# Eight-maxima gates, an earlier second half of f2, and expert 0's weights spread from token-major weights

## The chip, the cores and the metric

The kernel runs on one core of a Trainium2 chip. Such a core has TensorE (PE) for matrix products into PSUM banks, VectorE (DVE), ScalarE (ACT), GpSimd (POOL) and SyncE (SP), the last of which here only starts transfers. Each engine runs its own instructions in order and waits for others by semaphores. The metric is the time on the device in microseconds (us), the median of several runs; lower is better.

## The reference, cut to what matters

The program adds four blocks to a stream `x` of 8 batches of 100 tokens of width 256. Each block works on the layer norm of the stream and is weighted by the tanh of a gate: a cross attention, a top-1 mixture of experts, a text block with ternary weights (`bitnet_linear`: inputs rounded to 8 bits, one scale for the whole tensor), and a mixture-of-experts attention with 16 experts. The change lies at the end of the third block and in the start of the fourth:

```python
h = jax.nn.relu(bitnet_linear(concatenated, W_f1, b_f1))
return bitnet_linear(h, W_f2, b_f2)          # end of block 3; x = x + tanh(g) * this
# block 4, on x = layernorm(x), n = 800 tokens, E = 16 experts, MIN_E = 2
xn = x / jnp.maximum(jnp.linalg.norm(x, axis=-1, keepdims=True), 1e-12)
logits = xn @ sn - jax.nn.sigmoid(gates)
gated = jax.nn.relu(logits)
hard = (gated > 0).astype(gated.dtype)
inactive = jnp.sum(hard, axis=1) == 0        
_, fb_idx = jax.lax.top_k(logits, MIN_E)     # then the two best are put in
...
w = jax.nn.softmax(masked, axis=-1)          # over the active experts
y = jnp.einsum('nc,ech->neh', x, p)          # for p in q_proj, k_proj, v_proj
... = jnp.einsum('ne,neh->nh', w, y)
# then attention within a batch, and the 16 output projections, again weighted by w
```

## The kernel before

Block 4 is done in two halves of 4 batches (400 tokens, `HT`). The order on every engine is that of the code; there is no scheduler. Names ending in `_mm`, `_out`, `_in`, `_done` are semaphores.

**The layer f2.** The 8-bit form of h is made by `round_hidden` on VectorE and by a loop on ScalarE, one instruction for each of 8 row tiles and each half; `OWN` says how many tiles of each half VectorE takes (5 and 3), and ScalarE takes the others. `second_product(b)` multiplies batch b: one matmul for an offset, and eight over the tiles, which for b = 0 and b = 4 wait tile by tile. Its result goes to the bank and column of `RESULT[b]`. `third_residual(h)` adds the results to x on VectorE and takes statistics.

**The fourth norm and its turn.** `last_variance`, `last_normalise` and `token_norm` (VectorE) and `last_layernorm` (ScalarE) normalise; each engine does two batches of a half. `turn_half` transposes the normalised tokens on PE into two banks, and ScalarE copies these to `xT`.

**Gates.** `gate_scores` (PE) forms the logits, 100 tokens by 4x16. VectorE's `gate_logits`, `gate_second` and `gate_weights` make the weights w: the largest logit, the softmax's numerator, the second largest by masking the first out (ties go to the lower index, by a descending constant `rev16`), and the division. `link` makes an instruction's successors wait until it is through.

**Weights to the projections.** `turn_weights` transposes w to expert-major, ScalarE copies it to `wT`, and POOL stores it to DRAM and reads it back broadcast over 128 partitions (`w_bc`) in the groups of experts of `GROUPS`. Experts 0 and 1 of the first half do not wait for that: `spread_weights(e)` multiplies a broadcast unit column with `wT`, and VectorE copies the result to `w_bc` and multiplies the tokens with it straight from PSUM (`weigh_tokens`). `project(h, e)` adds expert e's three projections: 6 matmuls of 400 columns, which show as 12 rows in a trace, since a product in f32 is two instructions (a transpose is one). There are three buffers of weighted tokens (`NW`) and four of expert matrices (`NP`).

`keep_busy(bank, n)` is filler: n matmuls with constants whose result nobody reads. 

## Time and profile before

| | us |
|---|---|
| median of 3 runs | 611.05 |
| lowest, highest | 610.5, 611.07 |
| span of the profiled execution | 608.3 |

The profiled execution's own time is not given beside its span; the median is 2.75 us longer than the span.

| engine | busy us | share |
|---|---|---|
| PE, matmuls | 591.7 | 97% |
| DVE | 326.1 | 54% |
| ACT | 218.1 | 36% |
| POOL | 76.4 | 13% |

A row of a timeline gives the start, the time covered, the engine, the line of the code, the operation with its operands and shapes, and the count; in brackets the idle time ahead of it and what ended it. Filler counts as busy. The clock granted to PE is a share of full speed; the page's mean over the span is 0.992.

### The profile page before, as it was taken

The page shows a single profiled execution, that of the slowest core. Times are in us where ns is not written, and L with a number is a line of the kernel's source. Part 1 is how long each engine was busy: PE and PEld are TensorE (multiplying, and loading weights), DVE is VectorE, ACT ScalarE, POOL GpSimd, SP SyncE. Part 2 cuts the span into 40 slices and gives each one's busy share as a digit, 9 for nine tenths or more (in the row PEclk, how much of TensorE's full clock was granted, in tenths as well). Part 3 has the DMA queues.
Part 4 walks back from the last instruction along what each step waited for, and adds up shares of the span by engine and source line. Part 5 has one row for each costly group of instructions (what it writes and reads, how often), then busy time and mean ns, then how long its engine had stood idle before and what let it go on. Part 6 is the DMA issues. An engine that isn't in the chain of part 4 may idle for free.

```text
span 608.3 us, 9635 instructions
## 1 busy us (share of the span) xinstructions
PE 591.7 (97%) x3765; PEld 404.7 (67%) x3765; DVE 326.1 (54%) x787; ACT 218.1 (36%) x511; POOL 76.4 (13%) x75
## 2 busy tenths in 40 slices
PE   9999999999999989999999899999999999999997
PEld 7755344554556758999999568677655555555587
DVE  2896767697876664222222879976362223131454
ACT  3554665666664373111112575761200010001100
POOL 0052100022006102222231000001001000000000
PEclk9999999999999999999999799998999999999999
DMA  8910000102001645989994001501733833320000
GB/s 192 325 75 5 15 1 1 37 2 57 1 1 40 237 158 182 332 345 339 344 350 168 1 1 50 194 1 27 246 101 89 310 104 91 91 78 1 0 28 27
DMA packets 25580, 70.63 MB, mean 116 GB/s; under 512 B 5255, under 2 KB 13031, under 8 KB 21703
## 3 DMA queue, kind: packets, MB, share of 16 engines
q1 hardware_dynamic: 21910, 58.16, 29.0%
q0 software_dynamic: 3632, 11.97, 6.0%
q8 instruction: 25, 0.41, 0.3%
q14 instruction: 13, 0.10, 0.0%
HBM read 64.62 MB, written 5.49 MB: 115 GB/s over the span
## 4 chain that ended last, share of the span: by engine, by line
PE 84%; DVE 7%; ACT 5%; DMA 2%; issue 1%; POOL 1%; SPq 1%; DVEq 0%
PE bank L2115 21%; PE bank L1608 10%; PE bank L1935 8%; PE bank L1948 8%; PE bank L1761 7%; PE bank L2151 7%; PE bank L1735 5%; PE bank L1779 3%; DMA region<-in_ctxT 2%; PE bank L1704 2%; ACT region L1500 2%; PE bank L1767 2%; PE bank L2069 2%; PE bank L1589 1%; DVE nmax L1033 1%
## 5 line engine op out<-in xcount | busy, mean ns | idle before, releaser
L2115 PE MATMUL bank<-region,kvT 128*128 128x400 f32 x384 | 130.4, 500 | 0.0
L2115 PEld LDWEIGHTS bank<-region,kvT 128*128 128x128 f32 x384 | 72.4, 190 | 54.2 <-issue 0.3
L731 DVE TENSOR_REDUCE nmax<-bank 100x2 f32<-100x722 f32 x64 | 55.2, 905 | 24.9 <-PE bank L1735 24.6
L1174 DVE TENSOR_TENSOR region<-xT,stage 128x800 f32<-128x800 f32 x30 | 29.7, 991 | 70.0 <-PE bank L2115 69.9
L1935 PEld LDWEIGHTS bank<-stage,region 128*128 128x128 f32 x448 | 52.1, 192 | 1.4 <-issue 0.8
L1935 PE MATMUL bank<-stage,region 128*128 128x128 f32 x448 | 52.4, 275 | 0.5 <-ACT stage L1435 0.5
L1948 PE MATMUL bank<-region,stage 128*128 128x256 f32 x224 | 50.7, 379 | 0.0
L1948 PEld LDWEIGHTS bank<-region,stage 128*128 128x128 f32 x224 | 41.5, 190 | 5.1
L2151 PE MATMUL bank<-region,kvt 128*128 128x200 f32 (+1 forms) x192 | 44.5, 389 | 0.3 <-DVE region L1200 0.3
L1458 ACT ACTIVATE stage<-bank,stage 128x128 f32<-128x128 f32 x56 | 16.0, 368 | 66.5 <-PE bank L1935 61.1
L2151 PEld LDWEIGHTS bank<-region,kvt 128*128 128x128 f32 x192 | 33.5, 190 | 9.3 <-DVE region L1200 0.6
L947 DVE TENSOR_SCALAR stage<-bank,stage 128x128 f32<-128x128 f32 x56 | 15.8, 344 | 43.1 <-PE bank L1935 43.1
L1761 PE MATMUL bank<-xT,kvt 64*121 64x400 f32 (+1 forms) x144 | 37.9, 545 | 0.7 <-ACT region L1414 0.3
L1200 DVE TENSOR_TENSOR region<-region,stage 128x200 f32<-128x200 f32 (+1 forms) x48 | 20.5, 435 | 31.3 <-PE bank L2151 31.3
L1414 ACT ACTIVATE region<-bank 121x400 f32<-121x400 f32 (+1 forms) x48 | 21.8, 501 | 19.8 <-PE bank L1767 19.8
L1414 ACT ACTIVATE kvT<-bank 121x400 f32<-121x400 f32 (+1 forms) x48 | 21.8, 501 | 19.2 <-PE bank L1767 19.2
L953 DVE TENSOR_TENSOR stage<-bank,stage 128x256 f32<-128x256 f32 x14 | 5.9, 425 | 35.6 <-PE bank L1948 35.6
L1735 PE MATMUL bank<-kvt,xT 32*100 32x361 f32 x192 | 23.2, 502 | 1.2 <-POOL xT L473 0.7
L1761 PEld LDWEIGHTS bank<-xT,kvt 64*121 64x121 f32 (+1 forms) x144 | 13.3, 178 | 13.8 <-ACT region L1414 3.6
L1536 ACT ACTIVATE region<-bank 128x400 f32<-128x400 f32 x6 | 2.6, 504 | 55.5 <-PE bank L2115 55.5
L1608 PE MATMUL bank<-w_a,region 96*121 96x256 f32 (+1 forms) x96 | 22.1, 380 | 0.0
L1608 PE MATMUL bank<-region,w_a 96*128 96x361 f32 x64 | 21.2, 475 | 0.9 <-ACT xn L1327 0.7
(352 smaller groups left out, 932.2 us busy)
## 6 DMA issues: line engine op xcount, KB each, us to landing
region<-in_e_w SPq DMA_DIRECT2D x28, 1024.0 KB, 5.9
kvT<-in_p_qkv SPq DMA_DIRECT2D x32, 384.0 KB, 3.1
stage<-w_dram POOLq DMA_DIRECT2D x2, 1600.0 KB, 12.7
stage<-in_t_f SPq DMA_DIRECT2D x1, 2048.0 KB, 14.7
kvt<-in_p_o SPq DMA_DIRECT2D x1, 2048.0 KB, 9.6
stage<-in_e_b SPq DMA_DIRECT2D x14, 128.0 KB, 7.2
region<-in_ctxT SPq DMA_DIRECT2D x3, 541.5 KB, 14.3
stage<-w_dram POOLq DMA_DIRECT2D x1, 1200.0 KB, 8.8
```

What stands on the lines that cost most here:

```text
L731: dve.tensor_reduce(nmax[:, b % 2, at_h:at_h + 9:8], banks[0:N, bank:bank + 2, 0:M], AX.X, ALU.max, negate=True)\
L1174: dve.tensor_tensor(x_w[n % NW], xT[:, :, at_h], w_bc[h][:, None, e, :].to_broadcast([P, 2, HT]), ALU.mult).then_inc(S["xw_done"], 1)
L1200: dve.tensor_tensor(z_w[n % NW][:, at_p], oT[h][:, at_p], w_bc[h][:, e, at_p], ALU.mult)\
L1414: act.activation(probsT[n % 2][0:rows_c, c, g].rearrange("p j n -> p (j n)"), psum[4 + y % 3][0:rows_c, 0:4 * N], ACT.Exp).then_inc(S["y_o ...
L1608: ins = pe.matmul(bank, w(k), src(k), start=start and k == 0, stop=stop and k == kk - 1)
L1735: ins = pe.matmul(psum[i + (4 if b == 0 else 0)][0:N, 0:M], qm[b % 3][at_i, t, 2 * (i % 2) + par, :], kT[at_i, t, b, :], start=True, stop= ...
L1761: pe.matmul(bank[g], kT[at_g, t, b, c0:c0 + rows_c], qm[b % 3][at_g, t].rearrange("p j n -> p (j n)"), start=True, stop=False)
L1779: ins = pe.matmul(psum[7][32 * i:32 * i + VW, w * N:(w + 1) * N], v_b[b][0:rows_c, c, 8 * t + 2 * i + par, :], probsT[b % 2][0:rows_c, c, ...
L1935: ins = pe.matmul(psum[2 * u + m // 4][:, (m % 4) * P:(m % 4 + 1) * P], e_w1[u][:, k, m * P:(m + 1) * P], xsT[u][:, k, :], start=k == 0, s ...
L1948: ins = pe.matmul(psum[4 + u][:, 0:D], hsT[u][:, m, :], e_w2[u][:, m, :], start=m == 0, stop=m == KF - 1)
L2115: ins = pe.matmul(psum[3 * h + j][:, 0:HT], p_w[n % NP][:, k, j * HE:(j + 1) * HE], x_w[n % NW][:, k, :], start=e == 0 and k == 0, stop=e ...
L2151: ins = pe.matmul(psum[LAST_BANK[part] + m][:, at_p], o_all[:, e, m * P:(m + 1) * P], z_w[n % NW][:, at_p], start=e == 0, stop=e == E1 - 1)
```

## The change

- **Rounding.** `OWN` becomes (5, 0): ScalarE rounds all of the second half. f2's output scale is worked out on VectorE after its rounding, no longer ahead of it.
- **Products.** Seven of the eight f2 products stand ahead of the turn of the normalised tokens, with the banks of batches 4 to 7 exchanged; one stands behind the gate scores. The filler between the fourth product and the turn is gone.
- **Copy.** The second of the two turned banks of the first half is copied by VectorE.
- **Gates.** The largest eight logits of a token and their positions come from `max` and `max_index`, four of each per half (one per batch). The second gate is put in by comparing positions with a counting constant, to which 128 is added where the largest logit is above zero, so that then nothing matches.
- **Spreading.** `spread_weights` multiplies the token-major weights, one column broadcast to 128, with the identity: 4 matmuls of 100 columns in place of one of 400, and no need of `wT`. Expert 0's tokens are weighted in two parts, and `project_first` starts on the first, with expert 1's spreading between its halves. The rows of `w_bc` for experts 0 and 1 now come by a fourth broadcast on POOL's queue, which `weigh_heads` waits for.
- **A semaphore.** `w_2`'s load counts on the semaphore of `w_1`.

The first place is PE's queue around f2. Before, L2062 and L2069 are a product's offset and its eight tiles, L1589 filler, L2082 the turn, L1608 the gate scores:

```order
L2062 MATMUL bank<-stage 100x256
L2069 MATMUL bank<-tern,region 100x256 x8
L1589 MATMUL bank<-consts 128x256 x7
L2082 MATMUL bank<-consts,xn 128x100 x8
L1589 MATMUL bank<-consts 128x256
L1608 MATMUL bank<-sim,xT 100x16 x8
L2062 MATMUL bank<-stage 100x256
L2069 MATMUL bank<-tern,region 100x256 x8
L2062 MATMUL bank<-stage 100x256
```

After the change, from the fifth product on, the same things are on L2047 and L2054, L1575, L2067 and L1594:

```order
L2047 MATMUL bank<-stage 100x256
L2054 MATMUL bank<-tern,region 100x256 x8
L2047 MATMUL bank<-stage 100x256
L2054 MATMUL bank<-tern,region 100x256 x8
L2047 MATMUL bank<-stage 100x256
L2054 MATMUL bank<-tern,region 100x256 x8
L2067 MATMUL bank<-consts,xn 128x100 x8
L1575 MATMUL bank<-consts 128x256
L1594 MATMUL bank<-sim,xT 100x16 x8
L2047 MATMUL bank<-stage 100x256
L2054 MATMUL bank<-tern,region 100x256 x8
```

Three products have moved from behind the gate scores to ahead of the turn, in the place of seven filler calls.

The second place is PE's queue around the weights. Before, L2099 turns them, L2105 spreads, L2115 projects (18 calls are three experts):

```order
L2069 MATMUL bank<-tern,region 100x256 x8
L1589 MATMUL bank<-consts 128x256 x5
L2099 MATMUL bank<-consts,small 16x100 x4
L1589 MATMUL bank<-consts 128x256
L2105 MATMUL bank<-w_a,consts 128x400 x2
L1589 MATMUL bank<-consts 128x256 x2
L2115 MATMUL bank<-region,kvT 128x400 x18
```

After the change, the turn is on L2084, the spreading on L2091, expert 0's projection on L2101, the others' on L2114:

```order
L2054 MATMUL bank<-tern,region 100x256 x8
L1575 MATMUL bank<-consts 128x256 x4
L2084 MATMUL bank<-consts,small 16x100 x4
L2091 MATMUL bank<-consts,small 128x100 x4
L2101 MATMUL bank<-region,kvT 128x400 x3
L2091 MATMUL bank<-consts,small 128x100 x4
L2101 MATMUL bank<-region,kvT 128x400 x3
L2114 MATMUL bank<-region,kvT 128x400 x12
```

The fillers around the spreading are gone, and the second spreading has moved into the first projection.

The third place is VectorE's queue in the gates. Before, from the first comparison with zero; `r_a` to `r_d` are per-token numbers, `small` holds the logits and masks:

```order
L1113 TENSOR_SCALAR small<-small 100x64
L1114 TENSOR_REDUCE r_b<-small 100x4
L1115 TENSOR_SCALAR small<-small 100x64
L1116 TENSOR_TENSOR small<-small,r_b 100x64
L1117 TENSOR_SCALAR r_d<-r_b 100x4
L1118 TENSOR_TENSOR small<-small,r_d 100x64
L1120 TENSOR_REDUCE r_a<-small 100x4
L1121 TENSOR_SCALAR r_a<-r_a 100x4
L1132 TENSOR_TENSOR small<-small,consts 100x64
L1133 TENSOR_REDUCE r_b<-small 100x4
L1134 TENSOR_TENSOR small<-small,r_b 100x64
L1135 SCALAR_TENSOR_TENSOR small<-small 100x64
```

and 12 more follow until the weights are done. After, from the eight maxima on:

```order
L1113 MAX top<-small 100x8 x4
L1115 TENSOR_SCALAR small<-small 100x64
L1116 TENSOR_SCALAR r_d<-top 100x4
L1117 TENSOR_SCALAR far<-top 100x4
L1118 TENSOR_TENSOR small<-small,r_d 100x64
L1120 TENSOR_TENSOR small<-consts,far 100x64
L1122 TENSOR_SCALAR small<-small 100x64
L1124 MAX_INDEX top_at<-top,small 100x8 x4
L1131 TENSOR_TENSOR small<-small,top_at 100x64 x2
L1134 TENSOR_REDUCE small<-small 100x64
```

and 4 follow. The chain of linked small reductions has gone; MAX and MAX_INDEX stand four times each.

The diff, without the removed constant, the new tiles, the lists of semaphores and most of the removed `gate_second`:

```diff
--- before.py
+++ after.py
@@ -36,7 +36,7 @@
-OWN = (5, 3)
+OWN = (5, 0)
...
@@ -46,8 +46,8 @@
-RESULT = ((0, 0), (1, 0), (2, 0), (3, 0), (3, 0), (3, D), (6, 0), (6, D))
-GROUPS = (((2, 4), (4, 8), (8, 16)), ((0, 2), (2, 8), (8, 16)))
+RESULT = ((0, 0), (1, 0), (2, 0), (3, 0), (6, 0), (6, D), (3, 0), (3, D))
+GROUPS = (((2, 4), (4, 8), (8, 16), (0, 2)), ((0, 2), (2, 8), (8, 16)))
...
@@ -380,7 +382,7 @@
             sp.wait_ge(S["pv_mm"], 3)
-            sp.dma_start(w_2, d["w_2"]).then_inc(S["w1_small_in"], 16)
+            sp.dma_start(w_2, d["w_2"]).then_inc(S["ffn_in"], 16)
...
@@ -539,7 +541,7 @@
                 pool.wait_ge(S["wT_stored"], 16 * (h + 1))
                 for g, (e0, e1) in enumerate(GROUPS[h]):
                     pool.dma_start(w_bc[h][:, e0:e1], d["w_dram"][None, e0:e1, at_h].to_broadcast([P, e1 - e0, HT]))\
-                        .then_inc(S[f"wb_in{h}{g}"], 16)
+                        .then_inc(S[f"wb_in{h}{g}" if g < 3 else "wb_first"], 16)
...
@@ -1080,9 +1082,6 @@
             dve.tensor_reduce(scol[:, 20:21], umax[:, :], AX.X, ALU.max).then_inc(S["max_part"], 1)
             input_scale(6, 20)
             dve.sem_inc(S["in_scale"], 1)
-            output_scale(20, ("f2",))
-            link(dve.tensor_scalar(scol[:, 28:29], scol[:, 46:47], tg[:, 1:2], None, ALU.mult))
-
             def round_hidden(h, m):
 
...
@@ -1105,56 +1104,41 @@
             def gate_logits(h):
 
                 bs = slice(4 * h, 4 * h + 4)
-                lg_h, a_h, c_h = lg[:, bs, :], l_a[:, bs, :], l_b[:, bs, :]
+                lg_h = lg[:, bs, :]
                 dve.wait_ge(S["lg_mm"], h + 1)
                 link(dve.tensor_tensor(lg_h, psum[7 if h == 0 else 3][0:N, 0:4 * E1].rearrange("p (b e) -> p b e", b=4),
                                        nsq[:, bs, None].to_broadcast([N, 4, E1]), ALU.mult))
                 link(dve.tensor_tensor(lg_h, lg_h, sig[:, None, :].to_broadcast([N, 4, E1]), ALU.subtract))
-                dve.tensor_scalar(a_h, lg_h, 0.0, None, ALU.is_gt)
-                link(dve.tensor_reduce(r_b[:, bs], lg_h, AX.X, ALU.max))
+                for b in range(4 * h, 4 * h + 4):
+                    ins = dve.max(top8[:, b, :], lg[:, b, :])
+                link(ins)
                 dve.tensor_scalar(soft[:, bs, :], lg_h, 0.0, None, ALU.max)
-                dve.tensor_tensor(c_h, lg_h, r_b[:, bs, None].to_broadcast([N, 4, E1]), ALU.is_equal)
-                link(dve.tensor_scalar(r_d[:, bs], r_b[:, bs], 0.0, None, ALU.max))
+                dve.tensor_scalar(r_d[:, bs], top8[:, bs, 0], 0.0, None, ALU.max)
+                link(dve.tensor_scalar(far[:, bs], top8[:, bs, 0], 0.0, float(P), ALU.is_gt, ALU.mult))
                 dve.tensor_tensor(soft[:, bs, :], soft[:, bs, :], r_d[:, bs, None].to_broadcast([N, 4, E1]), ALU.subtract)\
                     .then_inc(S["lg_vec"], 1)
-                link(dve.tensor_reduce(r_a[:, bs], a_h, AX.X, ALU.add))
-                dve.tensor_scalar(r_a[:, bs], r_a[:, bs], 0.0, None, ALU.is_equal)
-
-            def gate_second(h):
+                dve.tensor_tensor(l_d[:, bs, :], const("slot", N)[:, None, 0:E1].to_broadcast([N, 4, E1]),
+                                  far[:, bs, None].to_broadcast([N, 4, E1]), ALU.add)
+                dve.tensor_scalar(l_a[:, bs, :], lg_h, 0.0, None, ALU.is_gt)
+                for b in range(4 * h, 4 * h + 4):
+                    ins = dve.max_index(top_at[:, b, :], top8[:, b, :], lg[:, b, :])
+                link(ins)
+
+            def gate_weights(h):
 
                 bs = slice(4 * h, 4 * h + 4)
-
-                def over(r):
-                    return r[:, bs, None].to_broadcast([N, 4, E1])
-
-                rev = const("rev16", N)[:, None, :].to_broadcast([N, 4, E1])
-                lg_h, first, second, rest = lg[:, bs, :], l_b[:, bs, :], l_c[:, bs, :], l_d[:, bs, :]
...
-            def gate_weights(h):
-
-                bs = slice(4 * h, 4 * h + 4)
-
-                def over(r):
-                    return r[:, bs, None].to_broadcast([N, 4, E1])
-
-                soft_h, a_h, put = soft[:, bs, :], l_a[:, bs, :], l_b[:, bs, :]
-                link(dve.tensor_tensor(put, put, over(r_a), ALU.mult))
-                link(dve.tensor_tensor(a_h, a_h, put, ALU.max))
+                for z in range(2):
+                    ins = dve.tensor_tensor(small[:, 2 + z, bs, :], l_d[:, bs, :],
+                                            top_at[:, bs, z:z + 1].to_broadcast([N, 4, E1]), ALU.is_equal)
+                link(ins)
+                link(dve.tensor_reduce(l_d[:, bs, :], small[:, 1:4, bs, :].rearrange("n z b e -> n b e z"), AX.X, ALU.max))
                 dve.wait_ge(S["lg_exp"], h + 1)
-                link(dve.tensor_tensor(soft_h, soft_h, a_h, ALU.mult))
+                soft_h = soft[:, bs, :]
+                link(dve.tensor_tensor(soft_h, soft_h, l_d[:, bs, :], ALU.mult))
                 link(dve.tensor_reduce(r_b[:, bs], soft_h, AX.X, ALU.add))
                 link(dve.reciprocal(r_b[:, bs], r_b[:, bs]))
-                dve.tensor_tensor(lg[:, bs, :], soft_h, over(r_b), ALU.mult).then_inc(S["w_done"], 1)
+                dve.tensor_tensor(lg[:, bs, :], soft_h, r_b[:, bs, None].to_broadcast([N, 4, E1]), ALU.mult)\
+                    .then_inc(S["w_done"], 1)
 
             def weigh_tokens(h, e):
 
@@ -1164,9 +1148,10 @@
                     dve.wait_ge(S["qkv_mm"], n - NW + 1)
                 if h == 0 and e < 2:
                     dve.wait_ge(S["w0_mm"], e + 1)
-                    dve.tensor_copy(w_bc[0][:, e, :], psum[4 + e][:, 0:HT])
-                    dve.tensor_tensor(x_w[n % NW], xT[:, :, at_h], psum[4 + e][:, None, 0:HT].to_broadcast([P, 2, HT]),
-                                      ALU.mult).then_inc(S["xw_done"], 1)
+                    for ks in (slice(0, 1), slice(1, 2)) if e == 0 else (slice(0, 2),):
+                        dve.tensor_tensor(x_w[n % NW][:, ks, :], xT[:, ks, at_h],
+                                          psum[4 + e][:, None, 0:HT].to_broadcast([P, ks.stop - ks.start, HT]), ALU.mult)\
+                            .then_inc(S["xw_done"], 1)
                     return
                 for g, (e0, _) in enumerate(GROUPS[h]):
                     if e == e0:
@@ -1195,6 +1180,8 @@
                 n, (h, at_p) = E1 * part + e, LAST_PART[part]
                 if e == 0 and part < 2:
                     dve.wait_ge(S["o_ready"], h + 1)
+                if n == 0:
+                    dve.wait_ge(S["wb_first"], 16)
                 if n >= NW:
                     dve.wait_ge(S["out_mm"], n - NW + 1)
                 dve.tensor_tensor(z_w[n % NW][:, at_p], oT[h][:, at_p], w_bc[h][:, e, at_p], ALU.mult)\
@@ -1209,14 +1196,15 @@
 
             for m in range(OWN[0]):
                 round_hidden(0, m)
-            for m in range(OWN[1]):
-                round_hidden(1, m)
+            output_scale(20, ("f2",))
+            link(dve.tensor_scalar(scol[:, 28:29], scol[:, 46:47], tg[:, 1:2], None, ALU.mult))
             third_residual(0)
             last_variance(0)
             last_normalise(0)
             token_norm(0)
+            dve.wait_ge(S["ln_turned"], 14)
+            dve.tensor_copy(xT[:, 1, 0:HT], psum[5][:, 0:HT]).then_inc(S["xT_ready"], 1)
             gate_logits(0)
-            gate_second(0)
             gate_weights(0)
             weigh_tokens(0, 0)
             weigh_tokens(0, 1)
@@ -1229,8 +1217,6 @@
                 weigh_tokens(0, e)
                 if e == 4:
                     gate_logits(1)
-                if e == 5:
-                    gate_second(1)
                 if e == 6:
                     gate_weights(1)
             for e in range(E1):
@@ -1516,7 +1502,7 @@
                 for b in range(4 * h + 2, 4 * h + 4):
                     act.activation(xn[:, b, :], x[:, b, :], ACT.Identity, bias=var[:, b:b + 1],
                                    scale=rstd[:, b:b + 1]).then_inc(S["ln_act"], 1)
-                for kk in range(2):
+                for kk in range(h + 1):
                     act.wait_ge(S["ln_turned"], 12 + 2 * h + kk + 1)
                     act.copy(xT[:, kk, h * HT:(h + 1) * HT], psum[(4 if h == 0 else 6) + kk][:, 0:HT])\
                         .then_inc(S["xT_ready"], 1)
@@ -1833,7 +1819,7 @@
                 if n == B:
-                    pe.wait_ge(S["ffn_in"], 32)
+                    pe.wait_ge(S["ffn_in"], 48)
                     pe.wait_ge(S["x_max"], 8 * B)
                     first_product(0, 0)
...
@@ -2057,7 +2042,7 @@
             def second_product(b):
 
                 bank, at = RESULT[b]
-                if b == 4:
+                if b == 6:
                     pe.wait_ge(S["x3_done"], 4)
...
@@ -2102,14 +2087,28 @@
 
             def spread_weights(e):
 
-                pe.matmul(psum[4 + e][:, 0:HT], ident[0:E1, e:e + 1].to_broadcast([E1, P]), wT[:, 0:HT],
-                          start=True, stop=True).then_inc(S["w0_mm"], 1)
+                for b in range(4):
+                    ins = pe.matmul(psum[4 + e][:, b * N:(b + 1) * N], lg[:, b, e:e + 1].to_broadcast([N, P]),
+                                    ident[0:N, 0:N], start=True, stop=True)
+                ins.then_inc(S["w0_mm"], 1)
+
+            def project_first():
+
+                pe.wait_ge(S["p_in0"], 16)
+                for k in range(2):
+                    pe.wait_ge(S["xw_done"], k + 1)
+                    for j in range(3):
+                        ins = pe.matmul(psum[j][:, 0:HT], p_w[0][:, k, j * HE:(j + 1) * HE], x_w[0][:, k, :],
+                                        start=k == 0, stop=False)
+                    if k == 0:
+                        spread_weights(1)
+                ins.then_inc(S["qkv_mm"], 1)
 
             def project(h, e):
 
                 n = E1 * h + e
                 pe.wait_ge(S[f"p_in{n % NP}"], 16 * (n // NP + 1))
-                pe.wait_ge(S["xw_done"], n + 1)
+                pe.wait_ge(S["xw_done"], n + 2)
                 for j in range(3):
                     for k in range(2):
                         ins = pe.matmul(psum[3 * h + j][:, 0:HT], p_w[n % NP][:, k, j * HE:(j + 1) * HE],
@@ -2166,23 +2165,20 @@
 
             pe.wait_ge(S["f2_sums"], 1)
             keep_busy(0, 7)
-            for b in range(4):
+            for b in range(7):
                 second_product(b)
-            keep_busy(6, 7)
             turn_half(0)
-            keep_busy(6, 1)
+            keep_busy(0, 1)
             gate_scores(0)
-            for b in range(4, B):
-                second_product(b)
-            keep_busy(0, 5)
+            second_product(7)
+            keep_busy(0, 4)
             turn_weights(0)
-            keep_busy(0, 1)
-            pe.wait_ge(S["wT_out"], 1)
             spread_weights(0)
-            spread_weights(1)
-            keep_busy(0, 2)
             for e in range(E1):
-                project(0, e)
+                if e == 0:
+                    project_first()
+                else:
+                    project(0, e)
                 if e == 2:
                     turn_half(1)
                 if e == 3:
```

## Rows read from the trace of the kernel before

**Rows 1.** The page: its head, and the engines' shares of the chain that ended last.
```profile
span 608.3 us, 9635 instructions
...
PE 84%; DVE 7%; ACT 5%; DMA 2%; issue 1%; POOL 1%; SPq 1%; DVEq 0%
```
**Rows 2.** Timeline of PE, 396 to 423 us.
```profile
396.45 3.19 PE L1589 MATMUL bank<-consts 128*128 128x256 f32 x14
...
407.69 1.42 PE L2082 MATMUL bank<-consts,xn 100*128 100x100 f32 x8
...
409.74 1.58 PE L1608 MATMUL bank<-sim,xT 128*100 128x16 f32 x16 [0.18 <-ACT xT L1521]
411.17 0.29 PE L2062 MATMUL bank<-stage 128*100 128x256 bf16 x1
...
412.89 0.42 PE L2062 MATMUL bank<-stage 128*100 128x256 bf16 x1
...
414.81 0.28 PE L2062 MATMUL bank<-stage 128*100 128x256 bf16 x1
...
416.79 2.32 PE L1589 MATMUL bank<-consts 128*128 128x256 f32 x10
418.95 0.51 PE L2099 MATMUL bank<-consts,small 100*16 100x100 f32 x4
...
420.03 1.60 PE L2105 MATMUL bank<-w_a,consts 16*128 16x400 f32 x4
...
422.61 12.33 PE L2115 MATMUL bank<-region,kvT 128*128 128x400 f32 x36
```
**Rows 3.** One microsecond within the products behind the scores, with the granted clock (PEclk).
```profile
core 0: us, PE busy (x) PEld busy (x) DVE busy (x) ACT busy (x) POOL busy (x), PEclk, DMA share, GB/s
412.00:413.00 1.00, 1.00 (x7) 0.97 (x6) 0.93 (x7) 0.00 (x0) 0.00 (x0) 0.50 0.00 0
```
**Rows 4.** Timeline of DVE, 399 to 428 us.
```profile
399.12 0.21 DVE L632 TENSOR_SCALAR scol<-ws,scol 128x1 f32<-128x1 f32 x1 [0.16 <-DVE scol L627]
...
399.62 2.79 DVE L1089 TENSOR_SCALAR region<-region,scol 128x400 bf16<-128x400 f32 x8
...
406.04 0.38 DVE L598 BATCH_NORM_AGGREGATE mv<-stats 100x2 f32<-100x6 f32 x4
...
411.44 0.23 DVE L1110 TENSOR_TENSOR small<-bank,nsq 100x64 f32<-100x64 f32 x1 [3.03 <-PE bank L1608]
...
411.95 0.20 DVE L1113 TENSOR_SCALAR small<-small 100x64 f32<-100x64 f32 x1
412.06 0.21 DVE L1114 TENSOR_REDUCE r_b<-small 100x4 f32<-100x64 f32 x1
412.31 0.20 DVE L1115 TENSOR_SCALAR small<-small 100x64 f32<-100x64 f32 x1
...
417.04 0.22 DVE L1157 TENSOR_TENSOR small<-small,r_b 100x64 f32<-100x64 f32 x1
421.00 0.57 DVE L1167 COPY stage<-bank 128x400 f32<-128x400 f32 x1 [3.73 <-PE bank L2105]
421.49 0.98 DVE L1168 TENSOR_TENSOR region<-xT,bank 128x800 f32<-128x800 f32 x1
...
423.76 0.87 DVE L1098 SCALAR_TENSOR_TENSOR x<-bank,scol,x 100x256 f32<-100x256 f32 x2
...
427.35 0.99 DVE L1174 TENSOR_TENSOR region<-xT,stage 128x800 f32<-128x800 f32 x1
```
**Rows 5.** Timeline of ACT: the rounding, and the copies of the turned tokens.
```profile
399.06 5.00 ACT L1506 ACTIVATE region<-region,scol 128x400 bf16<-128x400 f32 x8 [1.73 <-DVEq L1082]
...
408.80 0.89 ACT L1521 COPY xT<-bank 128x400 f32<-128x400 f32 x2 [0.40 <-PE bank L2082]
```
**Rows 6.** Chain that ended last: start, us, what; f32 matmuls of 128x128 elsewhere.
```profile
238.02 3.57 PE bank L1935 x32
```
**Rows 7.** Timeline of POOL: the broadcasts of the first half.
```profile
422.37 2.44 POOL L541 DMA_DIRECT2D stage<-w_dram  x3 [1.53 <-DMA w_dram<-w_a]
```

19 lines of the change are left out of this document (5 added, 14 removed).

## The prediction

> **What bounds the kernel now.** I read the page first: a span of 608.3 us, and a chain that ended last which is 84% TensorE [rows 1]. So time can come only from where TensorE waits or works on filler. The timeline of PE around the change shows both between the last text layer and the expert projections [rows 2]. Read it downwards: filler (L1589) until 399.47, the products of layer f2 (L2062, L2069), a second batch of filler, the turn of the normalised tokens at 407.69, the gate scores at 409.74, four more f2 products from 411.17, filler from 416.79, the turn of the gate weights at 418.95, the spreading at 420.03, and the first projection at 422.61. From there PE does not wait again until 556: the rows L2115 stand back to back, 36 instructions in 12.33 us or 0.34 us each. Whatever brings the start of expert 1's projection forward therefore comes off the end; what happens on VectorE or ScalarE counts only ahead of that point. The second half of the work (the second turn, scores and gates) lies under projections.
>
> One more thing is in [rows 2]: the four f2 products after the gate scores are not equal. The first takes 411.17 to 412.89 and the second 1.92 us, while the third and fourth take 0.99 us each (414.81 to 416.79). The row of that stretch says why [rows 3]: the granted clock is 0.50, so PE is at 1.2 GHz; it had just done the turn and the scores, many instructions with 100 or 16 columns and gaps. This costs before some 1.8 us on the path, and it is why the weights, finished on VectorE at 417.26 [rows 4], were picked up only at 418.95.
>
> **Part 1, rounding.** VectorE now rounds 5 tiles and computes f2's output scale behind them. The scale is known to both engines at about 399.06 (ACT starts then, [rows 5]), VectorE begins at 399.62 [rows 4]; the two small linked instructions between go behind, so rounding starts 0.5 us earlier. The first f2 product waits for the fifth tile, and the three behind it follow at 0.98 us each: all shift by 0.5, and the fourth product ends at 404.2, where a second batch of filler, now gone, stood behind it.
>
> **Part 2, three more products before the turn.** ScalarE now rounds 11 tiles instead of 8 at 5.00/8 = 0.625 us [rows 5]: the last is ready at 399.06 + 6.88 = 405.94. The fifth product wants it last, so PE waits some 0.8 us in it and goes on at 406.1. Two more products (0.99 each) end at 408.05. The normalised tokens would be ready for a turn at about 407.2 (407.69 less 0.5), the last of them at 407.9; so the turn starts 0.35 later than before but runs without its waits: 8 transposes took 1.42 us with waits, I take 0.86 without. That gives 408.9, plus 0.15 until the last result is out. ScalarE is free at 405.94, and wants to be by 406.1 for the standard deviations: covered by little.
>
> **Part 3, the copy of the turned tokens.** It took two ScalarE copies in sequence, 0.89 us from 408.80 [rows 5]. Now VectorE, idle there, does the second; 128x400 out of PSUM is 0.57 us [rows 4]. 409.05 + 0.57 + 0.05 gives gate scores at 409.70, before 409.74. Parts 1 to 3 together thus move the scores by nothing worth naming: the half microsecond and the parallel copy pay for three products moved ahead of them. VectorE's gates start at 411.40.
>
> **Part 4, what is left for PE behind the scores.** One product and 8 filler instructions (4 calls) instead of four products and 10. If the clock drops as before, the product ends at 412.85; filler takes 3.02/14 = 0.216 at full clock and twice that at half, so 4.5 of the 8 fit until 414.8 and the rest ends at 415.56. Without the drop it is 414.0.
>
> **Part 5, the gates on VectorE.** Before: 27 instructions in 5.82 us (411.44 to 417.26, [rows 4]), one linked to the next costing 0.25 us from start to start (412.06 to the next), one unlinked 0.11 (411.95 to 412.06), a small one in a row 0.07 (4 BN_AGGREGATE in 0.38). Now: two linked 0.51; four MAX over 16 values 3x0.08 + 0.25 = 0.49; three small 0.38; three 64-wide unlinked 0.39; four MAX_INDEX; two compares 0.39; a maximum over 3x64 values 0.39 (estimated from 0.21 at 64 elements and about 1 ns per further one, as 0.57 at 400 says); and the unchanged end, 0.95. MAX and MAX_INDEX have no row in this trace. The least is a small instruction's 0.07 to 0.08, the most the 0.57 us of the 128x400 copy [rows 4], far off in size. I take the near end, 0.08, and to be careful count an index operation double, since it has eight values to compare with besides the 16 it reads: 8x0.08 + 0.17 = 0.81. Sum 4.31 us, weights done at 415.71. With everything at 0.07 it is 0.1 less; at 0.25 for each of the 12 it would be 2.0 us more.
>
> A row cannot tell how many instructions an index operation is. The Trainium skill, "Vector Engine (DVE) Microarchitecture Reference", section 3.9, says that positions are found by a separate pair, one instruction that loads the eight values and one that searches: this speaks against the change by four instructions per half, some 0.3 us at the small row's pitch. By one instruction each, the weights would be done at 415.4.
>
> **Part 6, spreading without ScalarE.** Before, from the turn of weights to the first projection: turn 418.95, copy on ScalarE, spread at 420.03, VectorE at 421.00 copies (0.57) and multiplies (0.98), projection at 422.61: 3.66 us. Now the turn starts at 415.78 (weights at 415.71; PE has been free since 415.56) and takes 0.34. The spread of expert 0 follows at once: 4 calls, 8 f32 instructions; 32 such of 128x128 take 3.57 us [rows 6], 0.112 each, 0.89 together, out at 417.2. VectorE multiplies only half of the tokens' rows, 0.57, so PE starts at 417.94. The first projection then has the spread of expert 1 inside: 6x0.34 + 0.89 + 6x0.34 = 4.97, and expert 1's begins at 422.91. Before, it began at 422.61 + 12x0.34 = 426.69. **Gain: 3.78 us.** It comes from PE's queue (3.2 us earlier at the turn) and the shorter way (0.5 net of the spread in the projection).
>
> **What is late next.** Expert 1's tokens: its spread ends at 421.0, VectorE's 0.98 makes it 422.1, 0.8 in time. Then VectorE does the third residual's second half and statistics, 423.76 to 427.35 before [rows 4], now 422.05 to 425.65, and expert 2's product until 426.64; PE wants it at 422.91 + 4.08 = 426.99. In time by 0.3. Expert 2's weights come by POOL's DMA: issued 422.37 [rows 7] and read at 427.35 [rows 4], so at most 4.98 under way; now 3.2 us earlier, landed by 424.2. The extra load for experts 0 and 1 (400 KB) is last in POOL's queue for this half and wanted only after all 32 projections, 130 us later. Half 1's gates get shorter under cover: nothing. The load of w_2, now behind the same semaphore as w_1, is far ahead of its use: nothing. The 16 constant columns: nothing.
>
> **Sum.** The profiled span is 608.3 us; less 3.8 it is 604.5. The median of the runs is 611.05, 2.75 above the span, and I carry that: 611.05 - 3.8 = **607.2 us**.
>
> **Rivals.** (a) *The clock falls a second time.* Before, PE's stretch 415 to 422 was full of filler; now it is transposes, narrow spreads and 0.8 us of waiting before the projection. If the clock goes to half for as long as after the scores (411.2 to 414.8, 3.6 us), of which 3.5 fall on projections, these lose 1.75: gain 2.0, 609.0 us. For it: the drop seen came right after such work. Against: there is 1 us of filler at the start and a full projection from 417.94 on. The Trainium skill ("TensorE: Matmul & The Clock Gate", part 4) says that transposes don't count as PE being busy, which would make the four turns here idle time too and this rival more likely; nothing in the rows separates them from the 16-column scores. 13%. The same drop in the fifth product's wait (0.8 us) would halve two products and the turn: 609.6 us, 4%.
> (b) *MAX and MAX_INDEX are middling dear*, 0.2 us each: 1.3 us more, 608.5 us. For it: no row. 9%.
> (c) *Slower than before*: VectorE's gate chain becomes the bound by these twelve instructions. PE waits for it from the start, so each 0.1 us of price costs 1.2; the gain of 3.78 is eaten at 0.08 + 3.78/12 = 0.40 us each. At the far end, 0.57, it is 5.9 - 3.8 = 2.1 us slower, and PE's idle wait would bring the half clock as well, up to 1.75: 613 to 615. Against: they read 16 values, and a reduction over 64 values, linked, costs 0.25 [rows 4]. 4%.
> (d) *The gain is hidden*: expert 2's product or weights come late (0.3 us and 1.4 us in hand), PE stalls at 427 and gives back up to 3: about 610.2. 4%.
>
> **How the numbers follow.** The forecast has 66%, its own range 606.4 to 608.2: less time if the clock does not drop and VectorE is quick, more by small waits. The range 606.2 to 609.4 takes in (b) and most of (a). Within 0.2%, the least this kernel's measurement can tell, is 609.8 to 612.3: (d), a part of (a) and (c), 0.08; slower 0.04; faster 0.88.
>
> **What would show it.** In the profile after: rounding on VectorE from 399.1; a wait of about 0.8 us in the fifth product; scores at 409.7; MAX at 0.07 to 0.1 from start to start and the chain of gates about 4.3 us; filler ending just before the turn of weights at 415.8; spread at 0.11 per instruction; first projection at about 417.9 and then no wait of PE until the end. The forecast is wrong if the gate chain takes over 5 us, if the clock column shows a half behind 416, or if PE waits for VectorE at expert 2.

## The result

| | runs | median, us | lowest, highest |
|---|---|---|---|
| before | 14 | 611.06 | 609.3, 614.67 |
| changed | 14 | 609.14 | 607.66, 610.73 |

The ratio is 0.997, with a 95% interval of 0.9956 to 0.9983: faster by 1.9 us at the medians, 1.0 to 2.7 by the interval. The forecast was 607.2 with a gain of 3.8. The sign held, and 609.14 lies within the whole range of 606.2 to 609.4, but outside the 606.4 to 608.2 to which I had given 66%: the gain was half of what I worked out.

A puzzle stands at the start: the changed kernel's profiled execution, 610.73 us itself and the slowest of its 14, has a longer span than that of before.

```profile
span 608.9 us, 9618 instructions
...
PEclk9899999999999998999999899999999999999999
...
PE 84%; DVE 7%; ACT 5%; DMA 2%; issue 1%; SPq 1%; DVEq 0%; POOL 0%
```

The page's head, clock line and chain shares answer to [rows 1]. The timeline of PE in the same profile, from the filler behind f1 on, answers to [rows 2]:

```profile
401.16 3.19 PE L1575 MATMUL bank<-consts 128*128 128x256 f32 x14
...
410.66 0.31 PE L2054 MATMUL bank<-tern,region 128*100 128x256 bf16 x1 [0.19 <-ACT region L1492]
...
412.77 0.85 PE L2067 MATMUL bank<-consts,xn 100*128 100x100 f32 x8
...
414.36 1.58 PE L1594 MATMUL bank<-sim,xT 128*100 128x16 f32 x16 [0.28 <-DVE xT L1206]
415.79 0.29 PE L2047 MATMUL bank<-stage 128*100 128x256 bf16 x1
...
416.79 1.89 PE L1575 MATMUL bank<-consts 128*128 128x256 f32 x8
420.20 0.51 PE L2084 MATMUL bank<-consts,small 100*16 100x100 f32 x4 [1.52 <-DVE small L1140]
420.55 1.06 PE L2091 MATMUL bank<-consts,small 100*128 100x100 f32 x8
422.36 2.25 PE L2101 MATMUL bank<-region,kvT 128*128 128x400 f32 x6 [0.76 <-DVE region L1152]
...
427.36 8.22 PE L2114 MATMUL bank<-region,kvT 128*128 128x400 f32 x24
```

Two things are to be read here. The filler behind f1 starts at 401.16 where it started at 396.45 before: this execution had lost 4.7 us ahead of the stretch that the change is about. (Ahead of it the diff touches only the constants' table, theory C below, the semaphore of one load and the tiles reserved.) And from there to expert 1's projection it takes 26.20 us, where before it took 30.24 (396.45 to 426.69, by the working of part 6): the change did save 4.0 us in this stretch. Below, "the stretch" is measured from the start of f1's last matmul, 0.17 ahead of that filler, to the start of expert 1's first: 30.4 us in before's profile, 26.4 here. Behind it, every one of the 14 profiles that I have of all kernels here takes 181.5 us to its end, within 0.05. So the last part holds no loss and no gain.

The clock tells the rest. Before had its half clock behind the gate scores ([rows 3]); here it stays full there, so the one product takes 1.0 us and PE comes to the weights 1.52 us early. The view by windows shows it; its columns are the window, its length, then busy time and count of PE, PEld, DVE, ACT and POOL, the mean granted clock (1.00 is 2.4 GHz, 0.50 is 1.2 GHz), the DMA share and GB/s:

```profile
411.00:423.00 12.00, 9.45 (x75) 8.17 (x74) 6.86 (x37) 5.05 (x9) 0.57 (x1) 1.00 0.01 4
```

VectorE's gates, from the timeline of DVE in the changed kernel:

```profile
415.98 0.22 DVE L1109 TENSOR_TENSOR small<-bank,nsq 100x64 f32<-100x64 f32 x1 [1.68 <-PE bank L1594]
...
416.50 0.41 DVE L1113 MAX8 top<-small 100x8 f32<-100x16 f32 x4
416.94 0.20 DVE L1115 TENSOR_SCALAR small<-small 100x64 f32<-100x64 f32 x1
...
417.69 0.08 DVE L1124 MATCH_VALUE_LOAD top_at<-top,small 100x8 f32 x1
417.76 0.17 DVE L1124 FIND_INDEX8 top_at<-top,small 100x8 uint32<-100x16 f32 x1
417.85 0.07 DVE L1124 MATCH_VALUE_LOAD top_at<-top,small 100x8 f32 x1
...
418.40 0.36 DVE L1131 TENSOR_TENSOR small<-small,top_at 100x64 f32<-100x64 f32 x2
418.79 0.37 DVE L1134 TENSOR_REDUCE small<-small 100x64 f32<-100x192 f32 x1
...
419.92 0.22 DVE L1140 TENSOR_TENSOR small<-small,r_b 100x64 f32<-100x64 f32 x1
```

These rows answer to [rows 4]. The gates take 415.98 to 420.14, 4.16 us; four MAX take 0.44 from start to the next instruction, and each index operation is two instructions, 0.16 from one pair to the next (417.69, 417.85). The two that had no row, MAX and MAX_INDEX, were priced right.

So the question is not whether the 4.0 us are there, but where 2 of them go in the other executions.

### The profile page after: what moved, and what is told of

The parts are those of the page before. It is cut to its first block, busy times and chain, and to the rows that moved or that the text cites. A ratio compares the mean times of both kernels' runs of the same rounds, so it can differ in the third digit from the quotient of the medians.

```text
span 608.9 us, 9618 instructions
## 1 busy us (share of the span) xinstructions
PE 589.6 (97%) x3755; PEld 403.6 (66%) x3755; DVE 322.1 (53%) x786; ACT 220.1 (36%) x513; POOL 77.2 (13%) x76
## 3 DMA queue, kind: packets, MB, share of 16 engines
q1 hardware_dynamic: 21910, 58.15, 29.3%
## 4 chain that ended last, share of the span: by engine, by line
PE 84%; DVE 7%; ACT 5%; DMA 2%; issue 1%; SPq 1%; DVEq 0%; POOL 0%
PE bank L2114 21%; PE bank L1594 11%; PE bank L1920 8%; PE bank L1933 8%; PE bank L1747 7%; PE bank L2150 7%; PE bank L1721 5%; PE bank L1765 3%; DMA region<-in_ctxT 2%; PE bank L1690 2%; ACT region L1486 2%; PE bank L1753 2%; ACT region L1492 1%; DVE nmax L1035 1%; PE bank L1575 1%; DVE stage L1046 1%
## 5 line engine op out<-in xcount | busy, mean ns | idle before, releaser
L2114 PE MATMUL bank<-region,kvT 128*128 128x400 f32 x372 | 126.3, 500 | 0.0
L2114 PEld LDWEIGHTS bank<-region,kvT 128*128 128x128 f32 x372 | 70.2, 190 | 52.5
L1594 PE MATMUL bank<-region,w_a 96*128 96x361 f32 x64 | 22.9, 505 | 2.6 <-DMA region<-in_ctxT 1.9
L1594 PE MATMUL bank<-w_a,region 96*121 96x256 f32 (+1 forms) x96 | 22.1, 380 | 0.0
```

The lines of the kernel that those rows point to most:

```text
L1594: ins = pe.matmul(bank, w(k), src(k), start=start and k == 0, stop=stop and k == kk - 1)
L2114: ins = pe.matmul(psum[3 * h + j][:, 0:HT], p_w[n % NP][:, k, j * HE:(j + 1) * HE], x_w[n % NW][:, k, :], start=e == 0 and k == 0, stop=e ...
```

## The experiments

Three theories. **S**: the stretch saves 4.0 every time, and the scatter of what lies ahead of it hides this. **W**, named F in the first expectation: the saving itself differs between executions. It took its full form only after the first three runs: the stretch has more than one price in each kernel, by where the clock falls. Before is at 28.8, plus 1.6 when it falls behind the gate scores, as in its first profile; the changed kernel is at 26.4, plus up to 3 when it falls over the first projections, since PE waits twice just ahead of them. **C**: the constants' table, 16 columns shorter, makes the start slower. Each kernel ran 10 to 12 times, and one of these runs was profiled.

### Before, again

> The kernel before, unchanged: a second profile of it. Theory S (the change saves 4.0 us between the end of layer f1 and the projection of expert 1 in every execution, and the rest of what the times show comes from ahead of it): the stretch from the first filler behind f1 to the first row of expert 1's projection is 30.2 us again when the clock falls to half behind the gate scores, and about 28.7 when it does not, since PE then reaches the weights at 417.4 instead of 418.95. The span varies by what the start (transfers of the context, first 40 us) and the stretch 210 to 235 us cost. Rival F (the saving itself differs between executions): the stretch is 28.7 or less in this profile, so that the change is worth 2.5 or less in many executions.

611.36 us at the median of 10 (ratio to before 1.0012, 0.9986 to 1.0037). Its timeline of PE behind the scores:

```profile
418.56 2.32 PE L1589 MATMUL bank<-consts 128*128 128x256 f32 x10
420.75 0.51 PE L2099 MATMUL bank<-consts,small 100*16 100x100 f32 x4
...
424.42 5.95 PE L2115 MATMUL bank<-region,kvT 128*128 128x400 f32 x17
```

The scores began at 413.18, so the four products were through in 5.38 us with them; before's first profile took 7.05 (409.74 to 416.79, [rows 2]). The clock was full: the stretch is 28.8. So the half clock behind the scores is a matter of the execution, and with it 1.6 us of my gain: against this execution the change saves 2.4, not 4.0.

### Changed, again

> The changed kernel, unchanged: a second profile of it. Theory S: the same stretch takes 26.2 us again, whatever the clock does behind the scores. If the execution starts as that of before did (first transpose of the tokens at 23.6 and not 26.8 us) and has no half clock near 230, its span is about 604.5. Rival C (the shorter constants make the start slower): the first transpose is late again, near 26 to 27 us.

610.14 us at the median of 10 (0.9984, 0.9957 to 1.001). The stretch is 26.4. The first transpose of the tokens stands at 24.7; in the changed kernel's first profile it was at 26.8, in before's two at 23.7 and 24.1. So that slow start is not a fixed cost of the change (C). This profile alone cannot tell W from S.

### Changed, with the constants kept

```diff
-                  ("bounds", OVER), ("base", E0), ("rev8", E0), ("over", OVER),
+                  ("bounds", OVER), ("base", E0), ("rev8", E0), ("rev16", E1), ("over", OVER),
```

> The changed kernel with the 16 constant columns kept, so that the constants' transfer (128 x 620 numbers) and all addresses behind it are those of before. Rival C: the start is that of before (first transpose near 23.6) and the time is 2 us lower than the changed kernel's, about 607.2. Theory S: no difference, under 0.7 us either way.

608.7 us (0.9966, 0.9944 to 0.9989), which looked like C. But its profile shows what I had given 13%, here the timeline of PE:

```profile
416.32 0.51 PE L2085 MATMUL bank<-consts,small 100*16 100x100 f32 x4 [1.52 <-DVE small L1141]
416.67 1.06 PE L2092 MATMUL bank<-consts,small 100*128 100x100 f32 x8
418.48 4.34 PE L2102 MATMUL bank<-region,kvT 128*128 128x400 f32 x6 [0.75 <-DVE region L1153]
422.61 1.87 PE L2092 MATMUL bank<-consts,small 100*128 100x100 f32 x8
```

and the granted clock over it, in the view by windows for 417.8 to 424.6:

```profile
417.80:424.60 6.80, 6.12 (x15) 4.17 (x16) 1.10 (x3) 0.85 (x1) 3.56 (x5) 0.50 0.46 113
```

The six half products take 4.34 us in place of 2.25, and the spreading 1.87 in place of 1.03. PE is at 1.2 GHz for 6.8 us; before that it had waited 1.52 us and done narrow transposes and spreads, and the second wait, 0.75 us, had just begun (417.73). The stretch is 29.4: 3.0 more than without, more than the 1.75 of rival (a), since the fall lasted twice as long as the one I took it from.

### Only the new gates

```diff
-            gate_second(0)
...
-                if e == 5:
-                    gate_second(1)
```

with `gate_logits` and `gate_weights` of the changed kernel, all else of before.

> The kernel before with only the new gates (MAX and MAX_INDEX). The weights are done 1.5 us earlier on VectorE (4.2 instead of 5.8 us of chain), but PE's products and filler end at 418.95 relative to the same start, so the span stays: no difference within 0.3 us, unless the clock does not fall, where before is bound by filler too (417.4) and it is again 0.

611.07 us (1.0022, 0.9997 to 1.0047): no gain, as expected. The gates end 1.65 us sooner (4.17 against 5.82), and PE picks the weights up when its filler ends.

```profile
417.13 2.32 PE L1574 MATMUL bank<-consts 128*128 128x256 f32 x10
419.29 0.51 PE L2084 MATMUL bank<-consts,small 100*16 100x100 f32 x4
```

Its stretch is 30.4, with the half clock behind the scores again.

### More filler

```diff
-            keep_busy(0, 4)
+            keep_busy(0, 7)
             turn_weights(0)
             spread_weights(0)
+            keep_busy(0, 1)
```

> The changed kernel with three more filler calls ahead of the turn of the weights (7 instead of 4, in the 1.5 us in which PE waited for the weights when the clock was full) and one call behind expert 0's spreading (0.43 us, in the 0.76 us wait). Stretch = last row of f1's products to the first of expert 1's projection; it was 30.4 and 28.8 us in two profiles of before, 26.4, 26.4 and, in one with a half clock from 417.8 to 424.6, 29.4 in three of the change. Theory W (the changed order leaves PE so idle between 414 and 422 that in some executions the clock falls over the first projections, 3 us each time): no half clock there, the stretch is 26.4 to 26.6 or, where the clock falls behind the scores, up to 27.7; median time 0.5 to 1.5 us below the changed kernel's, ratio to before about 0.995. Rival S (the stretch always saves 4.0 and the rest is the start's scatter): no difference from the changed kernel, or slower by the filler.

608.53 us (0.997, 0.995 to 0.999), stretch 26.4, no half clock there. Its median is 0.6 and 1.6 below those of the changed kernel in its two earlier sets; none ran beside it: W's direction, but within the scatter.

### No filler

```diff
-            keep_busy(0, 4)
             turn_weights(0)
```

> The changed kernel without the 4 filler calls ahead of the turn of the weights: PE then waits 3.2 us there. Theory W: the clock falls over the projections in most executions; stretch about 29.4, median 2 us above the changed kernel's, near before's time. Rival S: the weights are the bound, the filler is only cover: stretch 26.4 and the same time.

612.18 us (1.0025, 1.0001 to 1.0049), some 3 us above the changed kernel's first median (from another set), though the kernel does less. The weights come as before; the wait for them is 3.25 us, and the clock falls ahead of the turn:

```profile
417.61 0.83 PE L2084 MATMUL bank<-consts,small 100*16 100x100 f32 x4 [3.25 <-DVE small L1140]
418.24 1.91 PE L2091 MATMUL bank<-consts,small 100*128 100x100 f32 x8
420.90 4.34 PE L2101 MATMUL bank<-region,kvT 128*128 128x400 f32 x6 [0.75 <-DVE region L1152]
```

```profile
415.70:425.90 10.20, 7.54 (x23) 5.25 (x24) 2.70 (x10) 1.76 (x2) 3.72 (x5) 0.50 0.25 55
```

Above is the timeline of PE, below it the same view by windows over the half clock, 10.2 us long. The stretch is 30.0. S is out, as it was with e3's 29.4: filler is not only cover here; without it the clock fell. The runs without a profile say the same: their mean clock over the span is 0.977 to 0.988 in all 12, where 28 of the 58 runs of the changed kernel (constants kept or not) have 0.989 or more.

### Only the f2 order

```diff
-            for b in range(4):
+            for b in range(7):
                 second_product(b)
-            keep_busy(6, 7)
             turn_half(0)
```

with the rounding, the copy and, up to the turn of the weights, the filler of the changed kernel; gates and spreading of before, with its fillers around the spreading.

> The kernel before with only the f2 order, the rounding, the copy and the fewer fillers; old gates and old spreading. By my terms: weights done at 5.8 us of chain (relative 417.2), turn there instead of 418.95, then the old 3.66 us to the projection with its fillers: stretch 28.8, 1.6 less than before where the clock falls behind the scores, 0 to 0.2 less where it does not.

614.47 us (1.0052, 1.0026 to 1.0079): slower than before by 3.4 at the medians (before has 611.03 in this set). The long gates now leave PE waiting 3.17 us, and the clock is at half from 421.9 to 428.7:

```profile
416.22 1.89 PE L1588 MATMUL bank<-consts 128*128 128x256 f32 x8
421.29 0.51 PE L2098 MATMUL bank<-consts,small 100*16 100x100 f32 x4 [3.17 <-DVE small L1154]
421.64 0.83 PE L1588 MATMUL bank<-consts 128*128 128x256 f32 x2
422.39 3.03 PE L2104 MATMUL bank<-w_a,consts 16*128 16x400 f32 x4
```

I expected a stretch of 28.8; it is 31.6. The turn comes 20.9 after f1's last matmul, and the 7.8 of the old way behind it (418.95 to 426.7 in before) would give 28.7: my terms hold, and 2.9 is the clock. It was a miss of the same kind as the prediction's.

### Gates and spreading, old f2 order

> The changed kernel with the old f2 order, rounding, copy and filler. PE's products and filler end when they did, so the turn is at the old place and the shorter gates give nothing; the new spreading saves 0.6: stretch 29.8 with a half clock behind the scores, 28.2 without. With e7: neither part alone gives the 4.0, the new gates pay only behind the new order. Theory W: filler up to the turn keeps the clock up over the projections, no half clock behind 417.

The changed kernel, with the rounding, the copy and the order of f2 as before; of its edit, the order:

```diff
-            for b in range(7):
+            for b in range(4):
                 second_product(b)
+            keep_busy(6, 7)
             turn_half(0)
...
-            second_product(7)
-            keep_busy(0, 4)
+            for b in range(4, B):
+                second_product(b)
+            keep_busy(0, 5)
```

610.83 us (1.0001, 0.998 to 1.0021), stretch 28.2, no half clock behind the scores nor over the projections: the second of the two expected values. Against before without a fall, 28.8, the new spreading gives 0.65 in the profile; the times do not show it, with an interval of 0.2% to either side.

### One set on one chip

The last four kernels ran side by side: the changed kernel as it is, the one with the constants kept (the edit shown above), the one with more filler (its edit shown above), and one with both edits.

The changed kernel:

> The changed kernel again, beside the three below on one chip. Theory W: the gain is 2.4 us without any fall of the clock around the change (28.8 to 26.4), 1.6 more where before has the fall behind the scores, and 3.0 less where the change has it over the projections; the mean of the times is 1.2 to 1.9 below before's. Its profile shows a stretch of 26.4 or, with a half clock from about 20 us behind the end of f1, 29.4, and nothing between.

608.78 us (0.9978, 0.9957 to 0.9998). This profile is the one to compare with [rows 2]: its last f1 matmul is at 396.33, before's at 396.28, so the two can be laid side by side to the end. Its span is 606.0 against 608.3.

```profile
409.71 1.58 PE L1594 MATMUL bank<-sim,xT 128*100 128x16 f32 x16 [0.28 <-DVE xT L1206]
412.14 1.89 PE L1575 MATMUL bank<-consts 128*128 128x256 f32 x8
415.56 0.51 PE L2084 MATMUL bank<-consts,small 100*16 100x100 f32 x4 [1.52 <-DVE small L1140]
415.91 1.06 PE L2091 MATMUL bank<-consts,small 100*128 100x100 f32 x8
417.72 3.82 PE L2101 MATMUL bank<-region,kvT 128*128 128x400 f32 x6 [0.75 <-DVE region L1152]
421.33 1.20 PE L2091 MATMUL bank<-consts,small 100*128 100x100 f32 x8
422.36 2.20 PE L2101 MATMUL bank<-region,kvT 128*128 128x400 f32 x6
424.40 5.87 PE L2114 MATMUL bank<-region,kvT 128*128 128x400 f32 x17
```

```profile
418.30:421.70 3.40, 3.40 (x8) 1.75 (x7) 0.00 (x0) 0.00 (x0) 2.69 (x4) 0.50 0.29 72
```

Above is the timeline of PE, below it the view by windows over the half clock. The half clock came here too, for 3.4 us: 1.7 lost, stretch 28.1. "Nothing between" 26.4 and 29.4 was wrong; how much is lost goes by how long it lasts and what it falls on. This fall came behind both waits, at 418.3, with the first two instructions of the projection already begun.

With the constants kept:

> The changed kernel with the 16 constant columns kept, again. It was 608.7 against 609.1 and 610.1 of the changed kernel in two sets, which the scatter of one execution (1 to 1.8 us) leaves open. Rival C (the shorter constants cost time in the start): again 0.8 or more below e9. Theory W: within 0.6 of e9.

609.98 us (0.9978, 0.9951 to 1.0005), 1.2 above the changed kernel beside it (0.9 in the means): more than the 0.6 that W allowed, and the opposite of C. Together the constants kept make 609.3 in the mean of 22 runs, the changed kernel 609.4 of 36: C is refuted. In the profile the half clock lies over the projections again (stretch 29.3). Timeline of PE and the view by windows:

```profile
417.82 0.51 PE L2085 MATMUL bank<-consts,small 100*16 100x100 f32 x4 [1.52 <-DVE small L1141]
418.17 1.06 PE L2092 MATMUL bank<-consts,small 100*128 100x100 f32 x8
419.99 4.34 PE L2102 MATMUL bank<-region,kvT 128*128 128x400 f32 x6 [0.76 <-DVE region L1153]
```

```profile
419.10:425.90 6.80, 6.04 (x17) 3.96 (x16) 1.05 (x2) 1.05 (x1) 3.71 (x5) 0.50 0.47 118
```

Here the clock is at half from 419.1, while the last of the spreading still runs (to 419.23): ahead of the second wait, which therefore was not needed for this fall.

With more filler:

> The changed kernel with 7+1 filler calls, again. Theory W: mean 0.7 to 1.3 us below e9 and no half clock over the projections in the profile (stretch 26.4). If the filler does nothing, it is within 0.5 of e9.

607.89 us (0.995, 0.9925 to 0.9976). Timeline of PE:

```profile
412.81 3.19 PE L1575 MATMUL bank<-consts 128*128 128x256 f32 x14
416.22 0.51 PE L2084 MATMUL bank<-consts,small 100*16 100x100 f32 x4 [0.23 <-DVE small L1140]
416.57 1.06 PE L2091 MATMUL bank<-consts,small 100*128 100x100 f32 x8
417.46 0.62 PE L1575 MATMUL bank<-consts 128*128 128x256 f32 x2
418.38 2.25 PE L2101 MATMUL bank<-region,kvT 128*128 128x400 f32 x6 [0.30 <-DVE region L1152]
```

The waits are 0.23 and 0.30 and the products take 2.25. Stretch 26.4, span 604.9.

With both:

> Both: 7+1 filler calls, constants kept. Theory W: as e11. Rival C: another 0.8 below e11, about 607.7.

608.02 us (0.9952, 0.993 to 0.9974), stretch 26.4: as e11, not 0.8 better.

### Taken together

| kernel | stretch in its profiles, us | mean of all runs, us (standard error) |
|---|---|---|
| before | 30.4, 28.8; 30.4 with the new gates | 610.9 (0.15), 125 runs |
| changed, constants kept or not | 26.4, 26.4, 28.1, 29.3, 29.4 | 609.35 (0.21), 58 runs |
| changed with 7+1 filler calls | 26.4, 26.4, 26.4 | 608.3 (0.27), 36 runs |

The means of the stretches are 29.9, 27.9 and 26.4: the second and third rows lie 2.0 and 3.5 below the first. By the means of the times it is 1.6 and 2.6. With so few profiles that is agreement in size, not more. (Of the five profiles in the second row, three are of the changed kernel, with 26.4, 26.4 and 28.1, and two of the one with the constants kept, with 29.4 and 29.3.) A second view needs no profile: each run gives the mean clock of its span. It does not tell where the clock fell, only how long in all: the profile of e11, with one half clock of 6.8 us (near 344), has 0.994, and before's, with one of 6.8 and one of 3.4 us, has 0.992. A clock of 0.993 or more was granted in 27 of 111 runs of before, in 2 of 58 of the changed kernel, and in 12 of 36 with the filler. And among the runs at 0.994 before has 608.9 (20 runs) and the filler version 606.6 (9 runs): 2.3 apart, close to the 2.4 between the stretches of 28.8 and 26.4.

The version with 7+1 filler calls beats both kernels: 0.995 to 0.997 of before in three sets, each interval below 1. It is 1.05 us (0.34) below the changed kernel over all runs, and 1.4 (0.5) on the one chip where both ran side by side (e9 and e10 against e11 and e12, 24 runs each).

## Where the prediction held and where it failed

Point by point, by its steps, laid on the profile that starts as before's did (e9):

| step | predicted | measured |
|---|---|---|
| rounding on VectorE starts | 399.1 | 399.18 |
| gate scores start | 409.70 | 409.71 |
| gates, length | 4.31 | 4.17 |
| turn of the weights | 415.78 | 415.56 |
| first projection | 417.94 | 417.72 |
| expert 1's projection | 422.91 | 424.40; 422.7 at full clock |

**Parts 1 to 3** held to 0.1 us. The fifth product took 0.95 us longer than its neighbours (404.22 to 406.15 against 0.98, in e9), where I gave 0.8, and was through at 406.15 against 406.1. **Part 4**: I allowed for a fall behind the scores; none of the nine profiles with the new order of f2 and filler behind it has one there, and in e9 the filler ended at 414.03, against the 414.0 that I gave for this case. **Part 5** held; the choice to count an index operation double was right: the Trainium skill ("Vector Engine (DVE) Microarchitecture Reference", section 3.9) has it as a loading and a searching instruction, and the trace agrees, with 0.07 and 0.09 us from one to the next (417.69, 417.76, 417.85). **Part 6** held: 2.09 + 0.87 + 2.04 = 5.00 us from start to start for the first projection with the spreading in it, by the changed kernel's rows (422.36, 424.45, 425.32, 427.36), against 4.97. (Its "0.5 net" for the shorter way should read 0.6: 3.17 + 0.61 are the 3.78.) **What is late next** held: no stall at expert 2, and nothing behind expert 1's projection differs.

The step that failed is the base of the sum: "This costs before some 1.8 us on the path". That is true of the profiled execution, and I carried it as a fixed cost of before, to be saved whole. A second profile did not have it: 1.6 of the 3.8 us are there in some executions only, and without them the change saves 2.4. The other term of the sum hid the same mistake. Every run whose span is on record took 1.8 to 1.9 us more than its span, not 2.75: the profiled execution was about 0.9 us quicker than the median one, in spite of the fall in its stretch, and so no picture of the median. The second failure is the price and chance of rival (a), "the clock falls a second time", 13% and 1.75 us: it was in three of five profiles (one of three of the changed kernel, at 1.7 us, and both with the constants kept, at 2.9 and 3.0). By the means of the profiles, few as they are, an estimate of the shares: some 0.5 us of the missing gain is before's base (30.4 against 29.9), and 1.5 is this rival (27.9 against 26.4), the larger part. Both errors have one source. I treated the clock as a property of the kernel, read from one profile, where it is a draw in each execution; the order of work only sets how often it falls and over what. The forecast was then right for the case that a fall in before meets none in the changed kernel, the best of the pairings; that the measured time still lay within the range owes something to its width, which took in a gain of 1.7.

I had named the cause of the rival: PE's fillers around the spreading were taken out. That waits of 1.5 and 0.75 us were left, right ahead of the densest part of the program, should have put it on a level with the forecast; the prediction counted only the second of them ("0.8 us of waiting before the projection"), since its filler ended just before the weights came. With the clock full behind the scores PE is there 1.5 us early. The filler of e5, e11 and e12 shortens these waits to 0.23 and 0.30, and none of the three profiles has a fall there.

Rivals (b) and (c) are refuted by the rows of MAX8 and FIND_INDEX8, (d) by the 181.5 us behind expert 1.

**What stays open.** Which of the two waits the filler has to fill: they were filled together. The falls point to the first, since e10's came ahead of the second wait and e3's 0.1 us into it (e9's came behind both); that filler in the first alone is enough is not shown. Whether 7+1 calls prevent the fall or only make it rarer: three profiles without it and the mean clocks say rarer at least. Why the clock falls in one execution and not in another of the same kernel. And what brings the falls ahead of f1: a half clock near 345 us is in all 14 profiles, others near 20 or between 213 and 233 us are in some, of before and of the changed kernel alike. They go with the scatter that hid the gain at first: f1's last matmul stood at 396.3 to 397.0 in the four profiles with 6.8 us of half clock ahead of it, at 397.1 to 399.0 in the four with 10 to 14 us, and at 399.0 to 401.0 in the six with 17 to 20 us. No experiment here touched those.

## What to carry to other kernels

Before a gain is counted from a profile, ask of each term whether it is of the kernel or of that execution: a stretch at half clock is of the execution until a second profile has it too. Filler that a faster partner makes needless as cover can still be needed for the clock; when a change opens waits of PE ahead of dense f32 work, give them back as filler, and compare the mean clocks of many runs of both kernels, which needs no profile. And a part that "gains" alone may lose alone: the f2 order cost 3.4 us without the shorter gates behind it.

## What the runs showed of the hardware

- MAX8 over 16 values on 100 partitions costs as little as a 4-wide instruction, 0.08 us from start to start; MATCH_VALUE_LOAD and FIND_INDEX8 together 0.14 to 0.16.
- A fall of the clock to 1.2 GHz on or just ahead of the f32 matmuls of 400 columns lasted 3.4 (e9), 6.8 (e3, e7, e10) or 10.2 us (e6) in these profiles. At half clock such a matmul starts every 0.67 us instead of every 0.34, so a microsecond of it costs half a microsecond where PE is busy: 3.4 us cost 1.7 in e9.
- The clock fell in some executions after a longest wait of 1.52 us (e3, e9, e10), and in before behind 16-column scores with no wait over 0.2 us in the 6 us ahead of it; other executions of the same kernels (e2, e1) kept it full there.
- Two executions of one unchanged kernel can differ by 5 to 8 us (608.0 to 615.6 for before in one set), with the mean clock ranging from 0.994 to 0.981 between them.
